# A four-layer graph attention kernel: the fourth layer turns its probabilities on VectorE in 32x32 blocks and weighs over 32 keys in eight array tiles; the second layer's key term goes in with the mask

## The reference

```python
x = _layernorm(x + _L0_gnn_ref(x, adj, ...))   # score_ij = sum_o W2_o relu(fa_i + fb_j), masked softmax over j, times x
x = _layernorm(x + _L1_gnn_ref(x, adj, ...))   # score_ij = sum_c yita_c leaky(vu_i + iv_j), softmax, times x, linear
x = _layernorm(x + _L2_gnn_ref(x, adj, ...))   # leaky(f1_j + f2_i), softmax over columns
# _L3_gnn_ref: 8 heads
scores = einsum('bmhd,bnhd->bhmn', q, k) * scale + edge_bias[edges]
scores = where(edges > 0, leaky_relu(scores, 0.2), -1e9)
attn = softmax(scores, axis=-1)
out = einsum('bhmn,bnhd->bmhd', attn, v).reshape(b, m, h * d) @ Wp + bp
```

## Time and profile before

| | before |
|---|---|
| median of 3 runs | 6071.91 us |
| the profiled execution's own time | 6070.47 us |
| its span in the trace | 6068.7 us |
| busy TensorE, VectorE, ScalarE, GpSimd | 5891.6, 5202.7, 5285.7, 650.7 us |
| mean granted clock of TensorE, share of full speed | 0.986 |
| second layer, eight row tiles of one graph | 255.4 us |
| fourth layer, first scores to the end | 1731.4 us |

### The profile page before, as it was taken

How to read it: one execution, slowest core, us unless ns; L and a number is a source line. 1 busy time by engine, 2 the same in 40 slices (tenths; PEclk the granted TensorE clock), 3 DMA queues, 4 the chain that set the end, 5 groups by cost and what they waited for, 6 DMA issues and landing times. The chain is left out here.

```text
span 6068.7 us, 131996 instructions
## 1 busy us (share of the span) xinstructions
PE 5891.6 (97%) x53828; PEld 2700.6 (45%) x53828; DVE 5202.7 (86%) x8890; ACT 5285.7 (87%) x6081; POOL 650.7 (11%) x441
## 2 busy tenths in 40 slices
PE   8999999999999999999999999987799999999999
PEld 2333333333333333333333333334576767767666
DVE  7999999999999999999999999966577777777777
ACT  7999999999999998989989899967588888888887
POOL 0000000000000000000000000013212112112121
PEclk9999999999999999999999999988799999999999
DMA  1000000000000000000000000015100000000000
GB/s 40 19 19 19 19 19 19 19 19 19 19 19 17 17 19 19 19 15 19 19 15 19 19 19 19 15 46 154 46 23 24 20 24 24 20 24 24 20 24 10
DMA packets 108872, 147.66 MB, mean 24 GB/s; under 512 B 15926, under 2 KB 83510, under 8 KB 108278
## 3 DMA queue, kind: packets, MB, share of 16 engines
q1 hardware_dynamic: 108278, 139.22, 7.3%
HBM read 137.10 MB, written 2.10 MB: 23 GB/s over the span
## 5 line engine op out<-in xcount | busy, mean ns | idle before, releaser
L253 ACT ACTIVATE a_hidden<-a_B,a_A 128x1024 f32<-128x1024 f32 x3200 | 3435.4, 1139 | 286.2 <-PE apsS L207 282.5
L329 DVE TENSOR_SCALAR a_hidden<-a_B,a_A 128x1024 f32<-128x1024 f32 x4992 | 3481.5, 766 | 198.0 <-PE apsS L207 172.7
L207 PE MATMUL apsS<-a_hidden,a_w_sel 128*32 128x512 f32 x32768 | 3561.4, 593 | 2.8 <-DVE a_hidden L329 2.8
L207 PEld LDWEIGHTS apsS<-a_hidden,a_w_sel 128*32 128x32 f32 x32768 | 1045.4, 110 | 2405.7 <-issue 2022.2
L699 ACT ACTIVATE Z<-m3S,bias 128x1024 f32<-128x1024 f32 x512 | 570.1, 1114 | 311.1 <-PE m3S L642 311.1
L749 DVE CUSTOM_DVE_ANT_0 Z<-Z,mask 128x1024 f32<-128x1024 f32 x512 | 624.9, 1221 | 122.5 <-ACT Z L699 120.2
L762 DVE COPY PT<-m3T 128x512 f32<-128x512 f32 x512 | 354.2, 692 | 322.2 <-PE m3T L654 321.6
L654 PE MATMUL m3T<-ident,Z 128*128 128x128 f32 x4096 | 565.3, 278 | 43.3 <-DVE PT L762 40.9
L707 ACT ACTIVATE Z<-Z,negm 128x1024 f32<-128x1024 f32 x512 | 589.1, 1151 | 12.0 <-DVE negm L755 12.0
L654 PEld LDWEIGHTS m3T<-ident,Z 128*128 128x128 f32 x4096 | 440.7, 141 | 285.2 <-issue 277.5
L119 POOL TENSOR_SCALAR a_mask<-a_adj_in 128x1024 f32<-128x1024 int32 x128 | 181.4, 1417 | 3439.4 <-DVE small L338 2951.0
(11 more groups left out here) (163 smaller groups left out, 2651.5 us busy)
## 6 DMA issues: line engine op xcount, KB each, us to landing
a_adj_in<-adj SPq DMA_DIRECT2D x128, 512.0 KB, 3.2
adj_in<-adj SPq DMA_DIRECT2D x128, 512.0 KB, 3.8
out<-yn SPq DMA_DIRECT2D x64, 32.0 KB, 1.5
wqT<-L_wqT SPq DMA_DIRECT2D x1, 130.0 KB, 2.8
wkT<-L_wkT SPq DMA_DIRECT2D x1, 130.0 KB, 2.9
wvT<-L_wvT SPq DMA_DIRECT2D x1, 130.0 KB, 2.8
wp<-L_gnn_Wp SPq DMA_DIRECT2D x1, 128.0 KB, 3.0
a_w_sel<-L_gnn_W SPq DMA_DIRECT2D x2, 0.2 KB, 6.7
```

The lines of the kernel that those rows point to most:

```text
L207: last = pe.matmul(psS[k % 2][32 * q:32 * q + 32, h * HALF:(h + 1) * HALF], w["sel"][layer][:, 30 - 2 * p:62 - 2 * p], hidden[:, (k * GROU ...
L253: act.activation(hidden[:, (k * GROUPS + p) % SLOTS, q, :], B2[:, g % 2, :], ACT.Relu, bias=A2[:, g % 2, pair:pair + 1]).then_inc(hid_act, 1)
L329: dve.tensor_scalar(hidden[:, (k * GROUPS + p) % SLOTS, q, :], B2[:, g % 2, :], A2[:, g % 2, pair:pair + 1], 0.0, ALU.add, ALU.max).then_i ...
```

## The change

**Second layer.** `key_term`, its split and its turning, and the two matmuls per row tile go. The key part is now made as rows that are equal on all 128 partitions: two matmuls of 512 columns per graph (`key_rows`), copied by ScalarE to `TB`. GpSimd adds it to each row tile's mask in a second instruction, so the add of the mask on VectorE brings it in.

```diff
+                m, row = k - nb * tiles, k // tiles % 2
+                if m < 0:
+                    gp.tensor_scalar(mask[:, k % 2, :], adj_in[:, k % 2, :], NEG, -NEG, ALU.mult,
+                                     ALU.add).then_inc(mask_ready, 1)
+                    return
                 gp.tensor_scalar(mask[:, k % 2, :], adj_in[:, k % 2, :], NEG, -NEG, ALU.mult,
-                                 ALU.add).then_inc(mask_ready, 1)
+                                 ALU.add).then_inc(mask_made, 1)
+                if m % tiles == 0:
+                    gp.wait_ge(aux_out, done("key_rows", k // tiles, 1))
+                gp.wait_ge(mask_made, m + 1)
+                gp.tensor_tensor(mask[:, k % 2, :], mask[:, k % 2, :], TB[:, row, :], ALU.add).then_inc(mask_ready, 1)
```

On TensorE:

```diff
-                elif what == "key_term":
-                    for t in range(tiles):
-                        last = pe.matmul(psA[:, t:t + 1], B2[0:C, g % 2, t * P:(t + 1) * P], w["u"], start=True, stop=True)
-                elif what == "turn_t":
...
+                elif what == "key_rows":
+                    last = pe.matmul(psA[:, :], w["u"], B2[0:C, g % 2, i * HALF:(i + 1) * HALF], start=True, stop=True)
...
-            def add_key_term(k):
...
-                pe.wait_ge(min_ready, k - 1)
-                for h in range(n // HALF):
-                    pe.matmul(psS[k % 2][:, h * HALF:(h + 1) * HALF], w["ones"], T3[:, g % 2, h * HALF:(h + 1) * HALF],
-                              start=True, stop=False)
```

```diff
+            def load_rows(b):
...
+                for a in range(4):
+                    for q in range(4):
+                        sp.dma_start(Xr[32 * a:32 * a + 32, b % 2, :].rearrange("p (t q c) -> p t q c", q=4, c=C)[:, :, q, :],
...
+            def scores(k, half):
...
+                at = 4 * k + 2 * half
+                if at >= 2:
+                    pe.wait_ge(leaky_ready, at - 1)
+                for e in range(2):
+                    rows = slice(C * e, C * e + C)
+                    last = pe.matmul(psS[(at + e) % 3][:, :], Q[rows, t % 2, h, :],
+                                     xT[rows, b % 2, half * HALF:(half + 1) * HALF], start=True, stop=True)
...
-            def turn(k, e):
...
-                    for j in range(4):
-                        at = (4 * side + j) * P
-                        last = pe.transpose(psT[:, side, j * P:(j + 1) * P], Z[:, k % 3, e, at:at + P], ident)
...
+            def weigh(p, chunk):
...
+                if chunk == 0:
+                    pe.wait_ge(turned, 2 * GROUP * (p + 1))
...
+                for step in (2 * chunk, 2 * chunk + 1):
+                    for a in range(4):
+                        rows = slice(32 * a, 32 * a + 32)
+                        for e in range(2):
+                            at = 2 * step + e
+                            last = pe.matmul(psO[C * e:C * e + C, a, :].rearrange("p (s c) -> p s c", s=2),
+                                             Xr[rows, b % 2, at * C:(at + 1) * C], ZT[rows, lo:hi + 1:hi - lo, at, :],
+                                             start=step == 0, stop=step == blocks // 2 - 1)
...
+                    p, c = divmod(2 * i + gap - 2 * GROUP - 3, 2 * GROUP)
+                    if 0 <= p < T // 2 and c < 8:
+                        weigh(p, c)
```

ScalarE, VectorE and GpSimd:

```diff
+                act.activation(Z(k, e)[:, half * HALF:(half + 1) * HALF], psS[(4 * k + 2 * half + e) % 3][:, :], ACT.Prelu,
...
-                act.activation(PT[:, k % 2, e, 0:HALF], psT[:, 0, :], ACT.Copy).then_inc(copied_low, 1)
...
+                dve.tensor_tensor_reduce(out=Z(k, e), in0=Z(k, e), in1=mask[:, m % 2, :], scale=1.0, scalar=-LOWEST,
+                                         op0=ALU.add, op1=ALU.min, accum_out=low[:, k % 4, e:e + 1]).then_inc(min_ready, 1)
...
+                at = 32 * (2 * h + e)
+                dve.transpose(ZT[:, m % 3, :, at:at + 32], Z(k, e).rearrange("p (b i) -> p b i", i=32)).then_inc(turned, 1)
...
+                gp.tensor_tensor(part[:, 0:4 * C], prod[:, 0:4 * C], prod[:, 4 * C:8 * C], ALU.add).then_inc(halved, 1)
```

More of the change, by code:

```diff
@@ L484, in _ @@
                 pe.matmul(psR[:, h:h + 1], wqT[:, h, 0:C], wkT[:, h, C:C + 1], start=True, stop=True)
-                pe.matmul(psW[side, pair * C:(pair + 1) * C], wvT[:, h, 0:C], wp[:, h, :], start=True, stop=True)
+                for g in range(2):
+                    pe.matmul(psW[C * g:C * g + C, h * C:(h + 1) * C], wvT[:, h, 0:C], wp[:, h, :], start=True, stop=True)
             pe.wait_ge(spread, 2)
@@ L521, in heads_layer, with held, part_of @@
+    adj_in, mask, ZT, OT, prod = buf["adj_in"], buf["mask"], buf["ZT"], buf["OT"], buf["prod"]
+    part, y, yn, den, low, rden = buf["part"], buf["y"], buf["yn"], buf["den"], buf["low"], buf["rden"]
+    stats, mv, vare, rstd, halfc = buf["stats"], buf["mv"], buf["vare"], buf["rstd"], small[:, 8:9]
+    Z = lambda k, e: Zs[2 * (k % 3) + e]
+    def held(p):
+        return sorted((2 * p % 3, (2 * p + 1) % 3))
+    def part_of(m):
+        return held(m // 2).index(m % 3)
     with ExitStack() as ctx:
@@ L554, in heads_layer @@
         order = list(first)
-        for k in range(U):
-            order += late_aux(k)
-        order += [("project", nb - 1, tiles - 1)]
+        for i in range(U + 2 * GROUP):
+            order += aux_jobs(i, 0) + aux_jobs(i, 1)
         place = {job: i for i, job in enumerate(order)}
@@ L603, in _ @@
+            for m in range(T + 5):
+                if m + 1 < T:
+                    make_mask(m + 1)
+                if m % 2 == 0 and 4 <= m < T + 4:
+                    add_heads(m - 4)
+                    add_heads(m - 3)
+                    normalise(m - 4)
+                    normalise(m - 3)
         @block.tensor
@@ L630, in aux @@
                                          start=True, stop=True)
                 last.then_inc(aux_made, 1)
-            def scores(k):
+            def scores(k, half):
                 b, s = divmod(k, SLOTS_B)
                 t, h = divmod(s, PAIRS)
-                if k >= 1:
-                    pe.wait_ge(leaky_ready, 2 * k)
-                pe.wait_ge(aux_out, done("query", b, t))
-                for half in range(2):
-                    for e in range(2):
-                        rows = slice(C * e, C * e + C)
-                        last = pe.matmul(psS[:, e, half * HALF:(half + 1) * HALF], Q[rows, t % 2, h, :],
-                                         xT[rows, b % 2, half * HALF:(half + 1) * HALF], start=True, stop=True)
-                last.then_inc(scored, 1)
@@ L657, in weigh @@
[L657 to L670 removed]
+                if half == 0:
+                    pe.wait_ge(aux_out, done("query", b, t))
@@ L739, in _, with masked_min @@
+            for i in range(U + 2 * GROUP):
+                for half in range(2):
+                    if i < U:
+                        leaky(i, half, 0)
+                        leaky(i, half, 1)
+                    if 1 <= i <= U:
+                        exponentials(i - 1, half)
+                    p, r = divmod(i - GROUP, GROUP)
+                    if 0 <= p < T // 2 and r in (6, 7):
+                        copy_o(p, 2 * (r - 6) + half)
         @block.vector
         def _(dve):
-            def masked_max(k, e):
+            def masked_min(k, e):
@@ L829, in _ @@
-            aux(("project", nb - 1, tiles - 1))
-            finish(T - 1)
-            normalise(T - 1)
+                    turn(i - 1, 0)
+                for job in aux_jobs(i, 0):
+                    aux(job)
+                if i < U:
+                    masked_min(i, 0)
+                    masked_min(i, 1)
+                if 1 <= i <= U:
+                    turn(i - 1, 1)
+                p, r = divmod(i - 2 * GROUP, GROUP)
+                if 0 <= p < T // 2 and r in (2, 3):
+                    deviations(2 * p + r - 2)
```

402 lines of the change are left out of this document (165 added, 237 removed).

## The result

The changed kernel takes 6100.68 us (median of 4 runs, 6097.11 to 6111.04) against 6072.66 us before: ratio 1.0051, 95% interval 1.0039 to 1.0063. It is slower, by 0.5%; the forecast was 5935 us. The profiled execution took 6111.04 us with a span of 6109.1.

What follows compares the result with a forecast made beforehand. TensorE's order was taken to bound both changed stages. From 6070.5 us, less 31 (second layer) and 107 (fourth), plus 1 for constants, came 5933, with the median's offset 5935; own range 5860 to 5995, wide range 5850 to 6110.

Steps and rivals of the forecast that it cites:

- TensorE's floor: Second layer: the least time TensorE needs per graph, 250.3 us after the change, from 255.4.
- the forecast's rule for the stall: Second layer: a GpSimd instruction of D us costs VectorE about D - 0.65; 1.5 us per addition.
- two level engines taking turns: Second layer: VectorE at 249.5 us and TensorE at 250.3 take turns, so a graph takes 251.5 us.
- Block transpose: Fourth layer, VectorE: one pass of 1.22 us per block transpose, with ends 0.75 and 2.44.
- rival (a): Fourth layer: the block transpose takes two passes, 2.2 to 2.44 us, and VectorE binds; kernel 6290 us, chance 0.09.
- Eight tiles at once: Fourth layer, TensorE: eight array tiles run together, so a weighing piece of 32 instructions takes 1.91 us.
- rival (b): Fourth layer: only four array tiles run at once, a piece taking 3.63 us; kernel 6370 us, chance 0.05.
- Half slots without weighing: Fourth layer: ScalarE needs 2.53 us and VectorE 2.49 per half slot; eight with helper work take 23.9 us a pair.
- The clock: I take 1.7 per pair: Fourth layer: TensorE's low clock mostly hides behind other engines and costs 1.7 us per pair, ends 0 and 9.
- rival (c): Fourth layer: low clock lasts through weighless half slots and first pieces behind, 9 us per pair; kernel 6167 us, chance 0.11.
- 1 for GpSimd: Fourth layer: GpSimd's 16 small instructions per pair meet VectorE's minima and cost 1 us, ends nothing and 5.
- the wide range: Whole kernel: 5850 to 6110 us, leaving out 0.17 above and little below.

Runs made afterwards that it cites:

- the spread version: The changed kernel with each tile weighed by itself over seven of every eight half slots, in 256-column instructions: 5835.99 us, ratio 0.9599.

## Why the prediction was wrong

**Second layer: right in the sum, by two errors that cancelled.** Gain 31 us forecast, 29 to 30 measured; TensorE's floor held (250.3 us forecast, 249.8 measured). The addition took 2.69 us and not 2.1, and its stall 2.1 and not 1.5, inside the bounds of 0.4 and 3.0; the forecast's rule for the stall (the length less 0.65) gives 2.04 for 2.69 and held. That is 5 us a graph more than forecast. The base to which it was added, 238.8 us of busy time, was too high for an engine that never waits: from the 251.0 us after, less eight stalls of 2.1, an estimate of what VectorE needed before is some 235 us with the split operations. So VectorE needs 251.0 for 249.5 forecast, and the pace of 251.3 is VectorE's alone, not two level engines taking turns.

**Block transpose: right.** 1.242 us for 1.22; rival (a) is out.

**Eight tiles at once: right.** From start to start a piece takes 1.91 us (5043.31 to 5045.22), the value taken; rival (b) is out. (The 28 instructions in 3.21 us that the forecast reads from the earlier trace rows stand in that trace at 2772.34, but not in those rows.) The scores ahead of it take 1.05 us (5042.26 to 5043.31) and not 0.96, half of the old eight: with four at a time the change of kind, 0.19, comes once for every four. That makes 2.96 us a half slot for 2.87, 0.7 us a pair.

**Half slots without weighing: right where nothing else disturbs them.** Slots 5 to 7 take 16.8 us where the forecast's terms make 17.8.

**"The clock: I take 1.7 per pair": the step that failed.** The mechanism was named, and the upper end of 9 covers it; the value did not. The reason given, that scores at half speed (1.8 us) still hide under 2.5, holds for scores alone. Slots 0 and 1 also hold a query, two projections and a piece of weighing, and at the low clock these do not hide: the query takes 1.70 us for 1.05 at full clock, a projection 3.65 for 1.97 (the rows for full clock are from the spread version):

```profile
5024.84 1.05 PE L623 MATMUL m3A<-xT,Wqk 64*128 64x128 f32 x8
5030.50 1.97 PE L630 MATMUL m3A<-Wvp,OT 128*128 128x64 f32 x16 [1.47 <-DVE Q L757]
```

With four halves of scores at 2.0 for 1.05 and a piece of weighing at 2.90 for 1.91, TensorE has 19.9 us of its own work in slots 0 and 1 at half speed and some 11 at full clock, an estimate from these rows. The forecast had 11.8 for the two slots, most of it at the pace of ScalarE and VectorE; at half speed TensorE sets the pace instead, busy for 19.55 of 20.61 us. So the overlap that the term assumed is what failed. Keeping the clock up for 506 of the 777 us gave 83 us of the kernel back, 2.6 us a pair, after the price of the unread matmuls and with a third of the low clock left; off slots 0 and 1 it took 4.5 a pair. The argument against rival (c), that scores alone would keep TensorE busy enough to end the low level, is refuted by the row 5018.00 to 5021.70, busy for 2.12 of 3.70 us and still at 0.50, and by the next one, busy for 8.95 of 10.00 and still at 0.50.

**A term that was missing: the handoff.** The forecast priced the helper groups by VectorE's work on them and put the wait between them at nothing. Three groups in three half slots in a row share one bank, and VectorE takes each out only in its own order. In the changed kernel the projections waited 36.7 us for it, 1.1 a pair of the 5 that the forecast missed. What it is worth there by itself no run shows, since the placing that removed it gave the scores a longer wait; in the spread version, at equal clock, one half slot of distance gave 59 us.

**The sum.** From the first to the last scores 1742 us passed for the forecast's 255 x 6.2 = 1581, and from there to the end 49.5 for 43: that is 161 + 6 of the layer's 1791 against 1624. Per pair: slots 0 and 1 take 8.5 us more than 11.8, slots 2 to 4 0.6 more, slots 5 to 7 1.1 less, and 2.7 were allowed for, the clock's 1.7 and 1 for GpSimd. That last term was of the right size by another path. Its sum over heads stretches the minima that it meets a little (1.27 and 1.33 us at 5040.33 and 5041.53, for 1.22), but 29 of the 512 ran beside the new mask instruction and took up to 2.05; in the kernel before no minimum was stretched:

```profile
L742 DVE CUSTOM_DVE_ANT_0 Z<-Z,mask x170: 1202/1223/2049, 4335.9 to 6060.8; 128x1024 f32<-128x1024 f32 x170
L749 DVE CUSTOM_DVE_ANT_0 Z<-Z,mask x512: 1212/1224/1227, 4342.5 to 6052.1; 128x1024 f32<-128x1024 f32 x171
```

**The chances.** What came, 6101 us, lies between rival (c) at half strength (6050) and at full (6167), joined by a wait that no rival had; the wide range reached up to 6110 and holds it, the forecast's own range to 5995 does not. (c) had 0.11; with a third layer in the trace of before that showed the clock falling in just such stretches, and a design that leaves TensorE half idle for half of each pair, that was too little.

## What to carry to other kernels

Work taken off the bound engine leaves holes; ask where they lie. Bunched, the weighing left 777 us of the layer at half speed, and the layer took 1791 us; spread evenly it left 175, and the layer took 1523; with the helper groups moved as well, 49 and 1370. When a helper result goes through one bank, count the time until the other engine, in its own order, takes it out, and leave that distance to the next user of the bank and to the first user of the result; here it took three half slots, and the scores waited 0.6 us for their query even then. An experiment that moves work also moves its cost: read the whole period, not only the slots that the work left. And where TensorE shows 100% busy, read the granted clock beside it before calling it the bound.

## What the runs showed of the hardware

- One unread matmul of 128x512 in six half slots a pair brought the low clock from 777 to 271 us, and gained 83 us in all: work without use was worth its price here, though spreading the weighing gave 265.
- Row and column tiles together do run eight at once in f32: a piece of 32 instructions, 32 deep, 64 wide and 512 columns long, takes 1.91 us from start to start at full clock, 2.90 where the clock changed on the way (5039.36 to 5042.26). With 256 columns the same number is 1.12 us busy for 1.97.
- A two-input addition of 128x1024 f32 on GpSimd took 2.69 us; the VectorE instruction of 0.743 us that met it lasted up to 2.88, a stall of 2.1 us.
- TensorE's low clock outlasted a stretch of work: in the changed kernel it was granted 0.50 for 10.00 us in which TensorE was busy for 8.95, and 0.54 over the next 10.60, in which it was busy throughout.
- The low clock in the third layer varied between profiles of kernels with the same third layer, from 142 to 196 us; from the last hidden matmul to the first scores it took 307.8 to 322.9.
